# The attention product of an AdaLN block as three fp32r products instead of one fp32 product

## The reference

```python
qkv = x @ w_qkv + b_qkv                       # x here: layernorm(x) * (1 + ca) + sa
scores = einsum('bhld,bhle->bhde', q, k) / sqrt(64)
attn = softmax(scores, axis=-1)
out = einsum('bhld,bhde->bhle', v, attn)
out = out @ w_fc + b_fc + x                   # then layernorm * gamma + beta
...
x = x + ga * attention(h)                     # called x2 in the kernel
h = layernorm(x) * (1 + cb) + sb              # called h2
xr, xk = mix(h, h of the position before)     # with mu_r, mu_k
x = x + gb * sigmoid(xr @ W_r) * (square(relu(xk @ W_k)) @ W_v)
```

## Time and profile before

| | us |
|---|---|
| median of 3 runs | 702.77 (701.91 to 705.32) |
| the profiled execution | 702.92 |
| its span | 701.3 |
| a batch of the loop | 81.5 |

### The profile page before, as it was taken

The page is one execution under the profiler, slowest core; times in us unless marked ns, Lnnn a source line. Parts: engine busy times, 40 slices in busy tenths (PEclk is TensorE's granted clock), DMA queues, the critical chain, the costliest instruction groups (busy, mean ns, idle before and its releaser), DMA issues.

```text
span 701.3 us, 11879 instructions
## 1 busy us (share of the span) xinstructions
PE 674.1 (96%) x3712; PEld 543.8 (78%) x3712; DVE 525.0 (75%) x1030; ACT 392.7 (56%) x871; POOL 389.6 (56%) x809
## 2 busy tenths in 40 slices
PE   7998999999999999999999999999999999998896
PEld 6777786978788887887869787888878878786665
DVE  4794898768888687867877688886878588467853
ACT  1424575556655575474755566554754747546553
POOL 5172885567275664586455672756635864326530
PEclk9989999999999999999999999999999999999999
DMA  9759245575946475573936758463765629626225
GB/s 313 226 158 220 90 135 114 112 182 97 212 80 149 125 157 120 97 165 95 215 85 122 170 111 196 89 148 115 157 120 98 123 56 203 114 38 149 31 30 90
DMA packets 90984, 93.02 MB, mean 133 GB/s; under 512 B 4224, under 2 KB 89000, under 8 KB 90960
## 3 DMA queue, kind: packets, MB, share of 16 engines
q0 software_dynamic: 33264, 33.03, 32.0%
q1 hardware_dynamic: 55344, 55.97, 25.3%
q10 hardware_dynamic: 2352, 3.73, 1.5%
HBM read 42.84 MB, written 33.10 MB: 108 GB/s over the span
## 4 chain that ended last, share of the span: by engine, by line
PE 35%; POOL 26%; issue 21%; DVE 9%; ACT 6%; POOLq 1%; DMA 1%; DVEq 0%; SPq 0%
PE work L1307 6%; PE att L1274 6%; PE gram L1256 5%; PE work L1324 4%; POOL x L483 4%; POOL ag L461 2%; ACT z L699 2%; POOL wv_aug L494 2%; PE tr L1249 2%; DVE mx L923 2%; POOL ag_a L461 2%; DVE t_buf L894 2%; POOL rs_o L478 2%; POOL wv_aug L497 2%; PE gram L1387 2%
## 5 line engine op out<-in xcount | busy, mean ns | idle before, releaser
L1274 PE MATMUL att<-m_sb,z_t 128*128 128x256 f32 x496 | 112.8, 380 | 8.0 <-DVE t_buf L894 7.2
L1274 PEld LDWEIGHTS att<-m_sb,z_t 128*128 128x128 f32 x496 | 92.3, 190 | 24.6 <-issue 13.4
L1324 PE MATMUL work<-mx,w_k_t 128*128 128x512 f32 x236 | 106.2, 592 | 0.0
L1307 PE MATMUL work<-w_r_t,mx 128*128 128x256 f32 x464 | 105.7, 381 | 0.0
L894 DVE SCALAR_TENSOR_TENSOR t_buf<-att,rs_o,g_row 128x256 f32<-128x256 f32 x124 | 51.4, 479 | 65.0 <-POOL rs_o L478 64.9
L1307 PEld LDWEIGHTS work<-w_r_t,mx 128*128 128x128 f32 x464 | 86.0, 190 | 11.0
L699 ACT ACTIVATE z<-x,ag 128x256 f32<-128x256 f32 x128 | 66.7, 601 | 48.8 <-POOL ag L471 48.8
L1256 PE MATMUL gram<-z 128*128 128x256 f32 (+1 forms) x512 | 90.5, 331 | 0.0
L449 POOL TENSOR_TENSOR ag<-st 128x4 f32<-128x4 f32 x32 | 18.7, 583 | 125.1 <-DVE st L905 125.1
L652 ACT ACTIVATE sq<-att 128x256 f32<-128x256 f32 x124 | 46.1, 384 | 72.6 <-PE att L1274 72.6
L1256 PEld LDWEIGHTS gram<-z 128*128 128x128 f32 x512 | 81.0, 194 | 6.9
(11 more groups left out here) (176 smaller groups left out, 1364.2 us busy)
## 6 DMA issues: line engine op xcount, KB each, us to landing
x_in<-in_L_attn_x_dram SPq DMA_DIRECT2D x32, 512.0 KB, 4.7
x<-rows SPq DMA_DIRECT2D x32, 512.0 KB, 3.5
x<-in_L_attn_x_dram POOLq DMA_DIRECT2D x32, 512.0 KB, 9.4
...
```

The costliest lines, as they stand in the source:

```text
L1274: ins = mm(att_banks(j, alone)[q][:, (t % 2) * D:(t % 2 + 1) * D], z_t[:, j, k, t * P:(t + 1) * P], m_sb[:, k], start=(k == 0), stop=(k == ...
L1307: ins = mm(r_banks(alone)[q][:, (t % 2) * D:(t % 2 + 1) * D], mixed(j, alone)[0][:, ch, tile], w_r_t[:, ch], start=(ch == 0), stop=(ch == ...
L1324: ins = mm(k_banks(alone)[dh][:], w_k_t[:, ch, rows_dh], mixed(j, alone)[1][:, ch], start=(ch == 0), stop=(ch == KD - 1))
```

## The change

**The product.** `attention` calls `mm3` on `z_hi`, `z_lo`, `m_hi`, `m_lo`: 24 fp32r products for a chunk in place of 8 fp32 ones.

**The parts of z.** ACT's copy out of `tr` now writes `z_hi` in fp32r (`copy_z_hi`). A new step on DVE, `low_z`, subtracts `z_hi` from the PSUM bank for `z_lo`, in two instructions for a chunk. The banks `tr` are free for the next transposes only after it: `turn_and_gram` and `turn_z2` wait for `z_lo_ready`, now for one bank at a time, where they waited for `z_t_ready`.

**The parts of M.** `make_m` on DVE goes on after `m_sb` with a copy to `m_hi` and a subtraction to `m_lo`, and `m_ready` comes after these.

**Room.** `k_hi` and `k_lo` have one buffer each instead of two; chunk 3 of the last batch uses `z_hi[:, 0]` and `z_hi[:, 1]` for them. `mixed` no longer uses `z_t` in the last batch, so the two last `mix` steps wait for the products that read the buffers before.

```diff
-        z_t = sb("z_t", [P, CH, KD, CT])
+        z_hi, z_lo = (part(n, [P, CH, KD, CT]) for n in ("z_hi", "z_lo"))
...
-        k_hi, k_lo = (part(n, [P, 2, KD, CT]) for n in ("k_hi", "k_lo"))
+        k_hi, k_lo = (part(n, [P, KD, CT]) for n in ("k_hi", "k_lo"))
...
-                    nc.scalar.activation(z_t[:, j, h], tr[h][:], ACT.Copy).then_inc(z_t_ready, 1)
+                    nc.scalar.activation(z_hi[:, j, h], tr[h][:], ACT.Copy).then_inc(z_hi_ready, 1)
...
+            def low_z(b, j):
+
+                i = CH * b + j
+                for h in range(KD):
+                    dve.wait_ge(z_hi_ready, 2 * i + h + 1)
+                    nc.vector.tensor_tensor(z_lo[:, j, h], tr[h][:], z_hi[:, j, h].bitcast(F32),
+                                            ALU.subtract).then_inc(z_lo_ready, 1)
...
-                                        res[:].rearrange("p k d -> p (k d)"), ALU.add).then_inc(m_ready, 1)
+                                        res[:].rearrange("p k d -> p (k d)"), ALU.add).then_inc(m_step, 1)
+                dve.wait_ge(m_step, 2 * b + 1)
+                nc.vector.tensor_copy(m_hi[:], m_sb[:]).then_inc(m_step, 1)
+                dve.wait_ge(m_step, 2 * b + 2)
+                nc.vector.tensor_tensor(m_lo[:], m_sb[:], m_hi[:].bitcast(F32), ALU.subtract).then_inc(m_ready, 1)
...
                 prep_now(n)
+                low_z(n, 0)
                 make_x2(b, 0)
...
-                            ins = mm(att_banks(j, alone)[q][:, (t % 2) * D:(t % 2 + 1) * D], z_t[:, j, k, t * P:(t + 1) * P], m_sb[:, k],
-                                     start=(k == 0), stop=(k == KD - 1))
+                            ins = mm3(att_banks(j, alone)[q][:, (t % 2) * D:(t % 2 + 1) * D],
+                                      (z_hi[:, j, k, tile], z_lo[:, j, k, tile], m_hi[:, k], m_lo[:, k]),
+                                      start=(k == 0), stop=(k == KD - 1))
```

More of the change, by code:

```diff
@@ L129, in adaln_block @@
         m_sb = sb("m_sb", [P, KD, D])
+        m_hi, m_lo = (part(n, [P, KD, D]) for n in ("m_hi", "m_lo"))
         x_in = sb("x_in", [P, CH, NT, D])
         z = sb("z", [P, 2, NT, D])
-        z_t = sb("z_t", [P, CH, KD, CT])
+        z_hi, z_lo = (part(n, [P, CH, KD, CT]) for n in ("z_hi", "z_lo"))
         st_a = sb("st_a", [P, CH, NT, 6])
@@ L158, in y_buf, with k_split, mixed @@
             return x_in[:, j] if alone else y[:, j % 2]
-        def k_split(j):
-            return k_hi[:, j % 2], k_lo[:, j % 2]
+        def k_split(j, alone):
+            return (z_hi[:, 0], z_hi[:, 1]) if alone and j == CH - 1 else (k_hi, k_lo)
         def o_banks(j, alone):
             return att if alone and j == CH - 1 else work[0:2]
-        def mixed(j, alone):
-            return (z_t[:, 2 * j - CH], z_t[:, 2 * j - CH + 1]) if alone and j >= CH // 2 else (xr[:, j % 2], xk[:, j % 2])
+        def mixed(j):
+            return xr[:, j % 2], xk[:, j % 2]
         wmod_sb = h2t[:, :, 1:1 + 6 * D]
@@ L251, in adaln_block @@
         z_used = sem("z_used")
-        z_t_ready = sem("z_t_ready")
+        z_hi_ready = sem("z_hi_ready")
+        z_lo_ready = sem("z_lo_ready")
         x2_rowed = [sem(f"x2_rowed{j}") for j in range(CH)]
@@ L683, in take_k @@
                     act.wait_ge(k_sq_ready, 2 * i + h + 1)
-                    nc.scalar.activation(k_split(j)[0][:, h], k[:], ACT.Copy).then_inc(k_hi_ready, 1)
+                    nc.scalar.activation(k_split(j, alone)[0][:, h], k[:], ACT.Copy).then_inc(k_hi_ready, 1)
             def prep_base_qk(b):
@@ L717, in row_steps @@
                     squares(b, 1)
-                    copy_z_t(n, 1)
+                    copy_z_hi(n, 1)
                 copy_h2(b, 0)
                 squares(b, 2)
-                copy_z_t(n, 2)
+                copy_z_hi(n, 2)
                 take_r(b, 0)
@@ L727, in row_steps @@
                 make_z2(b, 2)
-                copy_z_t(n, 3)
+                copy_z_hi(n, 3)
                 copy_gram(n)
@@ L770, in _ @@
             load_more()
-            copy_z_t(0, 0)
-            copy_z_t(0, 1)
+            copy_z_hi(0, 0)
+            copy_z_hi(0, 1)
             act.wait_ge(last_loaded, 16)
@@ L775, in _ @@
             copy_weights(0, [(wv_t[:, 0:2], att[0]), (wv_t[:, 2:4], att[1])])
-            copy_z_t(0, 2)
-            copy_z_t(0, 3)
+            copy_z_hi(0, 2)
+            copy_z_hi(0, 3)
             copy_gram(0)
@@ L906, in stats_2, with mix @@
                 ins.then_inc(st_2_done, 1)
-            def mix(b, j, made=None, alone=False):
+            def mix(b, j, made=None):
                 i = CH * b + j
-                if not alone:
-                    wait_past(dve, r_done, 2 * i - 2)
-                    wait_past(dve, k_done, 2 * i - 2)
+                wait_past(dve, r_done, 2 * i - 2)
+                wait_past(dve, k_done, 2 * i - 2)
                 wait_past(dve, xk_mixed, i)
@@ L920, in mix @@
                 dve.wait_ge(dif_done, i + 1)
-                for n, (dst, ready) in enumerate(zip(mixed(j, alone), (xr_mixed, xk_mixed))):
+                for n, (dst, ready) in enumerate(zip(mixed(j), (xr_mixed, xk_mixed))):
                     for h in range(KD):
@@ L1027, in row_steps @@
                     stats_a(n, 3)
+                    low_z(n, 1)
                     make_x2(b, 1)
@@ L1037, in row_steps @@
                 mix(b, 0)
+                low_z(n, 2)
                 if first:
@@ L1047, in row_steps @@
                 mix(b, 1)
+                low_z(n, 3)
                 gate_o(b, 0)
@@ L1086, in last_row @@
                 stats_2(b, 3)
-                mix(b, 2, alone=True)
+                mix(b, 2)
                 gate_o(b, 0)
                 low_k(b, 1, alone=True)
-                mix(b, 3, alone=True)
+                mix(b, 3)
                 gate_o(b, 1, alone=True)
@@ L1105, in _ @@
             make_z(0, 1, first=True)
+            low_z(0, 0)
             stats_a(0, 3)
@@ L1109, in _ @@
             prep_now(0)
+            low_z(0, 1)
             make_z(0, 3, first=True)
@@ L1112, in _ @@
             prep_qk(0)
+            low_z(0, 2)
             rows_b()
+            low_z(0, 3)
             centre_fc()
@@ L1238, in turn_and_gram @@
                 pe.wait_ge(z_ready, i + 1)
-                if first or j == 1:
-                    wait_past(pe, z_t_ready, 2 * i)
-                elif j == 0:
+                if j == 0:
                     wait_past(pe, h2_ready, 2 * CH * (b - 1))
-                else:
+                elif not first and j > 1:
                     pe.wait_ge(h2_ready, 2 * (CH * (b - 1) + j - 1))
                 for h in range(KD):
+                    if j > 0 and (first or j == 1):
+                        pe.wait_ge(z_lo_ready, 2 * i - 1 + h)
                     for t in range(NT):
@@ L1284, in turn_z2 @@
                     pe.wait_ge(t_done, CH * b + 2)
-                elif not last and j < CH - 1:
-                    pe.wait_ge(z_t_ready, 2 * (i + 1 + CH) + 2)
-                else:
+                elif last or j == CH - 1:
                     wait_past(pe, h2_ready, 2 * i)
                 for h in range(KD):
+                    if not last and j < CH - 1:
+                        pe.wait_ge(z_lo_ready, 2 * (i + 1 + CH) + 1 + h)
                     for t in range(NT):
```

20 lines of the change are left out of this document (11 added, 9 removed).

## The result

| | before | after |
|---|---|---|
| median | 704.37 us (701.91 to 705.32, 6 runs) | 711.26 us (708.87 to 713.06, 6 runs) |
| profiled execution, span | 702.92, 701.3 | 712.07, 710.5 |
| granted clock, mean | 0.989 | 0.981 |

The ratio is 1.0109, with a 95% interval of 1.0085 to 1.0132: the changed kernel is slower by about 1%, 6.9 us of the medians and 9.2 us between the two spans. The forecast was 707.0 with a range of 699.0 to 712.5. The direction is as forecast and the time lies in that range, though just above the 704 to 711 that the bounds of the terms gave; the growth, 6.9 us where 4.2 were forecast, is larger.

A forecast was written before the change was run, and what follows sets the result against it. PE, busy 96% of the span, was taken as nearly full, with one wait a batch on a DVE and POOL chain. Before batch 0 +2.3, batch 0 +2.1, loop +1.5, last batch -1.7: +4.2 us, 707.0, range 699.0 to 712.5.

The forecast's parts named there:

- the chain: Loop, from make_m over DVE and POOL to attention(b,2): the split of M delays it by +1.19 us a batch.
- the rival of the bare loads: In attention: weight loads not hidden, 24 products take 7.4 us a chunk, +126 us, 829 us; chance 0.01.
- the batch of the loop: Each loop batch: +1.19 - 2 x 0.62 + 0.3 = +0.25 us; six batches +1.5, bounds -1 and +5.
- the products of the second part: The two attention steps in the loop's 53.2 us of PE without a gap: each 0.62 us faster.
- low_z(n,3): Loop, before turn_z2(b,2): ends about 344.5, PE wants the bank at 344.6; hidden, by little, no cost.
- DVE waited for `z_hi`: Sign on DVE: a wait for z_hi makes the forecast wrong, as a late ACT and not the split then decides.
- the forecast of -1.7: Last batch: split hidden, no low_z, first three attention steps each 0.62 us faster; -1.7 us, bounds -2.5 and -0.6.
- Before batch 0: Ahead of the first batch: later wv_aug +1.1 and split of M +1.19, in all +2.3 us, bounds +1.2 and +3.9.
- batch 0: First batch: low_z on DVE delays PE and attention savings are lost in waits; +2.1 us, bounds +0.8 and +3.5.
- The low parts are absorbed: Rival: low_z costs nothing in loop batches, 1.0 us in the first batch; +0.5 in all, 703.4 us; chance 0.20.
- The split stays off the chain: Rival: DVE catches up before POOL needs stats_a(n+1,3); -5.3 us, 697.6 us, faster; chance 0.13.
- DVE becomes the bound: Rival: one low_z of each loop batch comes out bare, 1.26 us each, +7.6, 714.6 us; chance 0.12.

The follow-up runs named there:

- split_alone: Kernel before plus only the split of M on DVE, its parts read by nothing, attention still one fp32 product: 713.28 us, ratio 1.0150.
- before_stats_first: Kernel before with stats_a(n+1,3) put ahead of mix(b,3) on DVE, nothing else: 696.27 us, ratio 0.9907.
- product_stats_ahead: Changed kernel without low_z and split of M (three products on high parts only), stats_a(n+1,3) ahead of make_m(n) on DVE: 682.07 us, ratio 0.9706.
- product_alone: Changed kernel without low_z and split of M; three fp32r products on the high parts, both low parts missing from the result: 700.86 us, ratio 0.9965.
- no_low_z: Changed kernel without low_z, z_hi read in place of z_lo, split of M kept: 704.98 us, ratio 1.0029.
- stats_first: Changed kernel with stats_a(n+1,3) put ahead of mix(b,3) on DVE, nothing else: 704.43 us, ratio 1.0029.
- stats_ahead: Whole changed kernel with stats_a(n+1,3) put ahead of make_m(n) on DVE, nothing else: 694.52 us, ratio 0.9867.
- stats_ahead_low_later: Changed kernel with stats_a(n+1,3) ahead of make_m(n), low_z(n,0) behind low_k(b-1,3) and low_z(n,2) behind gate_o(b-1,3) in the loop: 689.13 us, ratio 0.9807.
- split_moved: Changed kernel with the split of M taken off DVE, ACT writing m_hi and POOL subtracting for m_lo: 710.99 us, ratio 1.0139.
- stats_first_low_later: Changed kernel with stats_a(n+1,3) ahead of mix(b,3), and in the loop low_z(n,0) behind low_k(b-1,3): 705.11 us, ratio 1.0043.
- low_z_alone: Changed kernel with one fp32 product on fp32 z and unsplit M; low_z runs but its result is unused: 706.34 us, ratio 1.0050.

## Why the prediction was right, and where it was not

**Right: the mechanism.** The product is faster on PE, a chain over DVE and POOL takes half of it, and the split of M lengthens that chain. split_alone showed the price, before_stats_first the chain, product_stats_ahead the gain behind it. The stage of `attention` costs 0.59 us less (forecast 0.62), with products 0.119 apart and not 0.117. The mix came 1.80 us after `m_sb` (1.80), the waits were 1.68 (1.8) and 1.43 (1.8), and `ffn_r(b,0)` took 0.24 longer (0.3).

**Right: the weight loads are hidden.** 24 products take 2.9 us beside 24 loads of 0.19: the rival of the bare loads is refuted here too. The rule of the Trainium skill (TensorE: Matmul & The Clock Gate, What overlaps and what doesn't, in The mechanism) would have made them bare; this trace too disagrees with it.

**Mis-sized: the batch of the loop,** +0.25 forecast, +0.7 in an undisturbed one. Its terms were
- the chain: +1.38, not +1.19. 1.18 arrived at `make_x2(b,0)`, as forecast; the other 0.2 came on POOL, between `stats_2(b,0)` and `rs_o(b,1)`. They stand in product_alone too, without any split, so they are not the split's. One of POOL's small instructions there takes 0.41 us where it took 0.19, though DVE makes z beside it in both kernels. Where it takes 0.41, it ends 0.06 us behind the last instruction of DVE's `make_z`, which had started some 0.05 us before it; in most batches of the kernel before that one starts after POOL's. That looks as if DVE held POOL up, but a few batches with POOL's 0.19 have DVE's start first as well, so it isn't settled.
- the products of the second part: -1.18, not -1.24.
- `low_z(n,2)` inside `ffn_r(b,0)`: +0.24, not +0.3.
- `low_z(n,3)`, "hidden, by little", was not: DVE waited 0.69 us for `z_hi` and the transposes of `turn_z2(b,2)` were held for 0.22 in the middle (the row at 350.21, 1.25 us long where others take 1.04).

1.38 - 1.18 + 0.24 + 0.22 = 0.66, and no_low_z bears out the last two: without `low_z` the batch is 0.50 shorter. This small error was made six times. The bounds (-1 to +5) held it, with 0.1 to spare.

**The signs that the prediction named.** It called itself wrong if DVE waited for `z_hi`. DVE did, for 4.4 us in each batch of the loop ahead of `low_z(n,1)`, where it had been idle before as well, and for 0.69 in four of the six ahead of `low_z(n,3)`. Of this only the 0.22 above reached PE, so the split still decides, and the sign was too broad. It also had PE's busy time fall by some 20 us, and it fell by 7.9. In a loop batch it fell by 1.36 (80.45 to 79.09) and not by 4 x 0.59 = 2.36: the view counts holds inside a stage, such as the 0.24 and the 0.22, as busy, and a stage at the lower clock is busy for longer. How the rest divides isn't worked out; the times are better read from stage to stage.

**Missing: the granted clock.** The prediction let PE's waits grow and took PE's speed as given in all the batches. One loop batch of six lost 1.0 us by it. In the last batch the gain was there (`turn_z2(7,3)` came 1.3 us nearer to the start of the batch than before), and the stretch behind its 2.87 us wait lost it again at a clock of 0.71. The kernel before had one such stretch in its last batch, behind the 2.92 us wait ahead of `turn_z2(7,2)` at 658.28, and the changed kernel has two: the first, behind the wait ahead of `turn_z2(7,1)`, only shortens PE's next wait, and the second, at the end, has no wait behind it that could take it. The nine kernels with the fp32r product bear this out. In the five with no such stretch behind PE's last long wait (product_alone, stats_first, product_stats_ahead, stats_ahead, stats_ahead_low_later) the last batch is 82.3 to 82.4 us, 1.3 to 1.5 less than before, which is near the forecast of -1.7; in the four with one (after, no_low_z, split_moved, stats_first_low_later) it is 83.6 to 84.2. So the term was right in mechanism, and the clock took it in this profile. Whether the clock also makes the changed kernel's times spread (708.9 to 713.1) isn't settled: the two executions with a mean granted clock of 0.981 took 712.1 and 712.8 us and one with 0.990 took 709.1, but one with 0.986 took 713.1.

**Before batch 0 and batch 0:** +1.45 and +2.6, inside their bounds, and in part by luck. Before batch 0 the split cost its 1.19, and `low_z` only 0.26 (`m_sb` at 57.45 against 57.19) where +1.1 was forecast: `wv_aug` was ready at 50.44 and not at 51.3, PE started its stage 0.60 later than before, and a higher clock took part of that back (2.35 us in place of 2.69). Other executions of the same code put `m_sb` up to 4 us later, as the table shows, so a term of this size can't be tested with one profile. In batch 0 low_z_alone gives +4.3, split_alone +1.1 and product_alone -0.7 from `m_sb` to `m_sb`. That adds up to 4.7, while the changed kernel has +3.7; it and low_z_alone each have one stretch at the lower clock in that batch, behind waits of 2.36 and 2.80 us, and what that costs isn't separated.

**The rivals.** "The low parts are absorbed" is right for the loop beside the fp32 product (low_z_alone: 81.57), right but for 0.5 us a batch beside the cheaper one (no_low_z), and wrong for batch 0. "The split stays off the chain" is refuted by split_alone, and "DVE becomes the bound" by low_z_alone and by the last kernel with its 85%.
